# Second attention: q and k projected transposed and passed through memory into the head stacks

## The reference, cut to what matters

```python
q = input_tensor @ wq.T + bq        # k, v alike; 16 heads of 16 channels
q = q.reshape(B, S, H, D).transpose(0, 2, 1, 3)
scores = jnp.einsum('bhsd,bhtd->bhst', q, k) / jnp.sqrt(jnp.float32(D))
attn = jax.nn.softmax(scores, axis=-1)
out = jnp.einsum('bhst,bhtd->bhsd', attn, v)
out = out.transpose(0, 2, 1, 3).reshape(B, S, E)
return out @ wo.T + bo
```

## Time and profile before

| | us |
|---|---|
| time, median of 3 runs | 2039.92 (2038.96 to 2041.53) |
| profiled execution, its time | 2040.23 |
| its span | 2038.5 |
| PE busy in the span | 1894.3 (93%) |
| DVE busy | 1445.4 (71%) |
| ACT busy | 1282.9 (63%) |
| POOL busy | 648.3 (32%) |

### The profile page before, as it was taken

One profiled execution on the slowest core, in us unless ns is written; L12 is line 12 of the kernel. 1 busy time (PEld: TensorE's weight loads), 2 busy tenths in 40 slices (PEclk: granted clock), 3 DMA queues, 4 the chain that ended last, 5 costly groups with the idle time before them and its releaser, 6 DMA issues. The chain is left out here.

```text
span 2038.5 us, 33530 instructions
## 1 busy us (share of the span) xinstructions
PE 1894.3 (93%) x12080; PEld 1465.6 (72%) x12080; DVE 1445.4 (71%) x2916; ACT 1282.9 (63%) x3061; POOL 648.3 (32%) x1021
## 2 busy tenths in 40 slices
PE   1999999999999999999999789997999999999997
PEld 1888878878888888787788568885555655655653
DVE  5785885886868868858768554445777777777773
ACT  3675674665756756746657465543777677777784
POOL 0353453543543534535435413221001111111112
PEclk9999999999999999999999999996999999999999
DMA  6110211111102111111111293321001011011001
GB/s 228 42 42 22 53 42 32 42 32 43 42 22 52 42 27 47 43 32 42 32 36 41 71 335 132 109 86 52 22 1 52 1 52 52 1 52 52 1 32 42
DMA packets 75204, 111.29 MB, mean 55 GB/s; under 512 B 8224, under 2 KB 49568, under 8 KB 74528
## 3 DMA queue, kind: packets, MB, share of 16 engines
q1 hardware_dynamic: 75040, 109.14, 18.3%
HBM read 54.59 MB, written 20.97 MB: 37 GB/s over the span
## 5 line engine op out<-in xcount | busy, mean ns | idle before, releaser
L1565 DVE TENSOR_REDUCE nm<-ps 128x1 f32<-128x512 f32 x512 | 337.0, 687 | 118.5 <-PE ps L1433 114.2
L1659 ACT ACTIVATE pt<-pst 128x512 f32<-128x512 f32 x512 | 296.8, 602 | 144.5 <-PE pst L1441 143.0
L805 POOL TENSOR_SCALAR pr<-pr,rinv 128x128 f32<-128x128 f32 (+3 forms) x512 | 263.1, 533 | 373.7 <-DVE rinv L693 373.7
L573 ACT ACTIVATE pr<-sc,nmax 128x128 f32<-128x128 f32 (+3 forms) x512 | 268.1, 527 | 142.3 <-DVE nmax L682 140.9
L682 DVE TENSOR_REDUCE nmax<-sc 128x1 f32<-128x128 f32 (+3 forms) x512 | 223.0, 484 | 75.4 <-PE sc L409 75.3
L1433 PE MATMUL ps<-kb,qb 96*128 96x512 f32 x512 | 239.8, 471 | 13.5 <-DVE nm L1565 11.2
L811 POOL TENSOR_TENSOR qk<-ra,rb 128x256 f32<-128x256 f32 x256 | 183.0, 735 | 206.8 <-DVE rb L704 171.7
L1441 PE MATMUL pst<-qb,kb 128*128 128x512 f32 x512 | 208.2, 408 | 6.8 <-ACT pt L1659 3.4
L1433 PEld LDWEIGHTS ps<-kb,qb 96*128 96x128 f32 x512 | 98.7, 193 | 145.3 <-issue 84.0
L421 PE MATMUL w<-ident,pr 128*128 128x128 f32 x1280 | 170.6, 280 | 25.6 <-DVE rb L704 19.7
L383 PE MATMUL w<-wq_hi,xt_hi 128*128 128x384 f32 x512 | 183.6, 359 | 2.8 <-DVE xt_lo L676 1.5
(11 more groups left out here) (212 smaller groups left out, 4552.9 us busy)
## 6 DMA issues: line engine op xcount, KB each, us to landing
k<-k SPq DMA_DIRECT2D x256, 128.0 KB, 2.2
raw<-in_w SPq DMA_DIRECT2D x16, 640.0 KB, 5.9
raw<-in_w SPq DMA_DIRECT2D x8, 704.0 KB, 4.2
xa<-in_x SPq DMA_DIRECT2D x2, 2048.0 KB, 13.7
x<-in_x SPq DMA_DIRECT2D x8, 512.0 KB, 3.9
x_scratch<-x SPq DMA_DIRECT2D x8, 512.0 KB, 2.9
xt_hi_scratch<-xt_hi SPq DMA_DIRECT2D x1, 4096.0 KB, 14.6
xt_lo_scratch<-xt_lo SPq DMA_DIRECT2D x1, 4096.0 KB, 23.8
```

The lines of the kernel that those rows point to most:

```text
L573: act.activation(pr[:, h, SOFF[i]:SOFF[i] + (i + 1) * P], sc[:, bank, at:at + (i + 1) * P], ACT.Exp, bias=nmax[:, h, i:i + 1], accum_out=r ...
L805: pool.tensor_scalar(p, p, rinv[:, h, i:i + 1], 1.0, ALU.mult, ALU.mult).then_inc(scaled, 1)
L1565: dve.tensor_reduce(nm[:, g % 2, i, h:h + 1], ps[:, i % 2, :], AXX, ALU.max, negate=True).then_inc(max_done, 1)
L1659: act.activation(pt[:, g % 2, h, i, :], pst[:, i % 2, :], ACT.Exp).then_inc(exp_done, 1)
```

## The change

q and k are projected transposed: the weights are now the stationary operand and the tokens the moving one (`project_z`), 128 channels by 512 tokens to a piece. A piece s is q (0) or k (1) of half u of the heads; n = 2b + u counts the halves. ACT adds the bias and rounds (`round_z`), DVE makes the remainder in one instruction (`rest_z`), and SP writes each part to where it belongs in a scratch tensor `z1` in memory, six DMAs a half (`store_z`), and reads a group's stacks from there, four DMAs a group (`load_stacks`). The zero halves of `kb` are set once, on DVE and POOL ahead of the loop. v is projected as before in pieces of 256 columns (`project_v`, `take_v`). `split_z`, `turn_z`, `take_stack`, `own` and `qn` are gone. One of the two copies of the maxima goes from DVE to ACT, the selector copies too. In `experts` only q and k of the first half of batch row 0 are projected.

```diff
+def project_z(pe, c, n, s, out, xs):
+    cols = slice(s * C + n % 2 * P, s * C + n % 2 * P + P)
+    for k in range(NC):
+        pe.matmul(out, c.w1h0[:, k, cols], xs[0][:, k, :], start=(k == 0), stop=False)
+        pe.matmul(out, c.w1h0[:, k, cols], xs[1][:, k, :], start=False, stop=False)
+        mm = pe.matmul(out, c.w1l0[:, k, cols], xs[0][:, k, :], start=False, stop=(k == NC - 1))
+    mm.then_inc(c.z_done, 1)
+def round_z(act, c, n, s, src):
+    act.wait_ge(c.z_done, 2 * n + s + 1)
+    if n > 0:
+        act.wait_ge(c.z_stored, 96 * n)
+    act.activation(c.zt[:, 0, s, :], src, ACT.Identity, bias=c.bz[:, 2 * s + n % 2:2 * s + n % 2 + 1], scale=1.0).then_inc(c.zt_hi_done, 1)
+def rest_z(dve, c, n, s, src):
+    dve.wait_ge(c.zt_hi_done, 2 * n + s + 1)
+    dve.scalar_tensor_tensor(out=c.zt[:, 1, s, :], in0=src, scalar=c.bz[:, 2 * s + n % 2:2 * s + n % 2 + 1],
+                             in1=c.zt[:, 0, s, :].bitcast(F32), op0=ALU.add, op1=ALU.subtract).then_inc(c.zt_lo_done, 1)
+def store_z(sp, c, io, n):
+    for s, parts in enumerate(((0, 1, 0), (0, 0, 1))):
+        sp.wait_ge(c.zt_hi_done, 2 * n + s + 1)
+        sp.wait_ge(c.zt_lo_done, 2 * n + s + 1)
+        for r, part in enumerate(parts):
+            dst = io.z1[n % 2, s].rearrange("h (r d) t -> h r d t", d=D1)[:, r]
+            sp.dma_start(dst, c.zt[:, part, s, :].bitcast(F32)).then_inc(c.z_stored, 16)
...
-        TURNS = ((0, 0), (0, 1), (0, 3), (1, 1))
-        STACKS = ((0, 0), (0, 1), (0, 3), (1, 0), (1, 1), (1, 2))
-        PROJECTIONS = ((1, 3), (2, 0), (2, 2), (2, 3))
+        Z_PE, Z_ACT, Z_DVE = ((0, 2), (2, 0)), ((0, 3), (2, 1)), ((1, 1), (2, 2))
+        V_PE, V_DVE = ((1, 0), (1, 3), (2, 1), (2, 3)), ((1, 1), (2, 0), (2, 2), (3, 0))
+        O_PE, O_DVE = ((0, 2), (1, 1), (2, 0), (2, 3)), ((0, 3), (1, 2), (2, 1), (3, 0))
...
+                def load_stacks(q):
+                    n, g = q // 2, q % NG1
+                    sp.wait_ge(c.z_stored, 96 * n + 96)
+                    if q < NG1:
+                        sp.wait_ge(kz_pool, g + 1)
+                    else:
+                        sp.wait_ge(st_done, 16 * (q - NG1) + 16)
...
+                        sp.dma_start(qb[rows, g].bitcast(F32), zq[e]).then_inc(stack_in[g], 16)
+                        sp.dma_start(kb[rows, g].rearrange("p (a e) t -> p e a t", e=2)[:, e].bitcast(F32), zk[e]).then_inc(stack_in[g], 16)
...
+                for b in range(B):
+                    if b < B - 1:
+                        store_half(b + 1, 0)
+                        load_stacks(NG1 * (b + 1))
+                        load_stacks(NG1 * (b + 1) + 1)
+                        store_half(b + 1, 1)
+                        load_stacks(NG1 * (b + 1) + 2)
+                        if b < B - 2:
+                            load_xs(b + 2)
+                        load_stacks(NG1 * (b + 1) + 3)
+                    if b > 0:
+                        store(b - 1)
+                        load_xg(b)
...
+                            if g % 2 == 0 and (h, i) in Z_PE and not last:
+                                project_half(b + 1, g // 2, Z_PE.index((h, i)))
+                            if g == 1 and (h, i) in V_PE and not last:
+                                project_v(b + 1, V_PE.index((h, i)))
+                            if g == 3 and (h, i) in O_PE and not first:
+                                out_project(b - 1, O_PE.index((h, i)))
...
-                    for a in range(2):
-                        dve.tensor_copy(qb[2 * S3:P, g, a, :], pn[2 * D1 * a:2 * D1 * (a + 1), :]).then_inc(n_done, 1)
+                    dve.tensor_copy(qb[2 * S3:P, g, 0, :], pn[0:2 * D1, :]).then_inc(n_dve, 1)
...
+                            if g == 2 and h == 0 and i < NC and not first:
+                                split_ot(b - 1, i)
...
+                pool.memset(kb[0:2 * S3, 0, HG // 2:HG].bitcast(F32), 0.0).then_inc(kz_pool, 1)
+                for g in range(1, NG1):
+                    pool.memset(kb[0:2 * S3, g].bitcast(F32), 0.0).then_inc(kz_pool, 1)
```

More of the change, by code:

```diff
@@ L1084, in _ @@
                     ffn(e, e % 2, last=e == E1 - 1)
+                act.wait_ge(a_bias_done, 1)
+                for s in range(2):
+                    round_z(act, c, 0, s, w[:, s, :])
             @block.vector
@@ L1162, in _ @@
                     ffn(e, e % 2, last=e == E1 - 1)
[L1164 to L1169, removed]
+                for s in range(2):
+                    rest_z(dve, c, 0, s, w[:, s, :])
             @block.tensor
@@ L1384, in finish @@
                         pool.tensor_tensor(x1[:, i, :], x1[:, i, :], so[:, i % 2, :], ALU.add).then_inc(x_done, 1)
-                def row(b, first=False, last=False):
-                    for g in range(NG1):
-                        if not (last and g > 0):
-                            split_z(b + (g + 3) // NG1, (g + 3) % NG1)
-                        if g == 2 and not first:
-                            finish(b - 1)
-                for g in range(3):
-                    split_z(0, g)
                 for b in range(B):
-                    row(b, first=b == 0, last=b == B - 1)
@@ L1493, in group @@
                     back1, back2 = (not (first and g < n) for n in (1, 2))
-                    projects = g == 1 and not last
                     for h in range(HG):
@@ L1531, in group @@
+                            if h == HG - 1 and i == 1 and more1:
+                                turn_n(q + 1)
+                            if h == HG - 1 and g == 1 and not first and i >= 2:
+                                turn_on(b - 1, i - 2)
                         if back1:
                             weigh(q - 1, (g + 3) % NG1, h, b + 1 if g else b)
-                for j in range(4):
-                    turn_z(0, j, (qn_done, 2 * NT) if j < 2 else (stack_done, j - 1))
                 for n in range(HG + 1):
@@ L1641, in _ @@
                         maximum(0, 0, h, i)
+                        if h == 1:
+                            take_v(0, i)
+                        if h == 3 and i < 2:
+                            rest_z(dve, c, 1, i, w[:, i, :])
                 split_n(0, 0)
@@ L1650, in _ @@
                     take_o(q, q % NG1)
-                split_ot(B - 1)
+                for k in range(NC):
+                    split_ot(B - 1, k)
                 for i in range(NT):
@@ L1699, in group @@
                     q = NG1 * b + g
-                    more2, more3 = (not (last and g + n >= NG1) for n in (2, 3))
+                    more1 = not (last and g + 1 >= NG1)
                     back2 = not (first and g < 2)
```

304 lines of the change are left out of this document (129 added, 175 removed).

## The result

| | before | after |
|---|---|---|
| median, us | 2040.72 | 2009.99 (2008.04 to 2013.04) |
| ratio | 1 | 0.9853 [0.9841, 0.9865] |
| profiled execution, us | 2040.23 | 2010.16 |
| its span, us | 2038.5 | 2008.4 |
| DMA traffic, mean over the span | 55 GB/s | 81 GB/s |

The account below looks back on a forecast made before the run. PE looked full, but a ring of two score banks was taken to set each step's floor of 3.55 us. 2040.2 - 45.5 (seven rows) - 3.6 (last row) - 3 (start) = 1988 us, range 1966 to 2010.

Parts of the forecast that it names:

- the term of -3: Start of the attention stage: between -5 and +3 us, taken as -3, nearer to full clock.
- The round trip: Start: stacks stored to memory and loaded back, two transfers of 3 to 7 us each, for scores from about 1395.
- Wrong if PE waits for DMA in the loop: Sign against the forecast, in the attention loop: stack loads were expected hidden, about 15 us of queue against some 30.
- The clock at the start: First group at full instead of half clock, 2.5 us less, since transposes don't count as clock activity.
- the ring of two banks: Each attention step: two score banks passing between PE and the maxima set a floor of 3.55 us, not PE's work.
- Rival A: Whole loop: PE's work sets the time and every removed transpose counts, giving 1968 us, a row 67.6; chance 0.12.
- rival B: Loop: new DVE work holds up maxima, gain only 2 to 4 us a row, 2016 us; chance 0.14.
- C: Loop: stacks come late from memory; at 35 us PE waits 5 us four times a row, 2128; 0.09 with D.
- D: Loop: granted clock falls to 1.2 GHz, 14 us a group, 2044 to 2100 us; chance 0.09 together with C.
- (b): Loop: ACT loses stack copies and casts, POOL its subtractions; counted as nothing by itself.
- the 16 transposes: Each group's transposes of q and k removed: 0.56 us per bundle of four, 9.0 us of PE a batch row.
- (c): One of two casts of the maxima moves from DVE to ACT, removing a wait of 0.55 us before h=0.

Follow-up runs that it names:

- e2: Changed kernel with project_z of batch row 0's first half moved into the last expert's down projection and its stores ahead of the last gate stores: 2008.54 us.
- e4: Changed kernel with the edits of e1 and e2 together: 1993.0 us, ratio 0.9765.
- e3: Changed kernel with k's three of the six first-half z stores issued from ACT's queue instead of SP's: 2009.09 us, ratio 0.9845.
- e7: Changed kernel with scratch rows reordered so the 128 rows of a z store lie at one pitch, not in 8 blocks: 2000.45 us.
- e8: Changed kernel with the edits of e1, e2 and e7, and each gate store cut in two of 64 rows: 1982.55 us, ratio 0.9715.
- e9: As e8, but with project_z of batch row 0 left behind the last down projection: 1981.26 us, ratio 0.9715.
- e1: Changed kernel with load_xs(1) issued on SP's queue ahead of row 0's second-half stores and the stacks of groups 2 and 3: 1997.17 us.
- e10: Kernel before, with ACT copying only 8 of 512 columns of each q and k stack from the fifth group on: 2030.96 us, ratio 0.9952.
- e6: Kernel before, with only one of four transposes in each q and k bundle made from the third group on: 2025.76 us, ratio 0.9929.
- e5: Changed kernel with both casts of the maxima on DVE again, none on ACT: 2019.73 us, ratio 0.9899.

## Why the prediction was right and where it was wrong

**The step that failed is the start, the term of -3, measured +20.4.** Some 1.2 us of it were there before the stage (its first projection starts at 1378.05 before and at 1379.24 after). That is within what single executions differ by: e2 and e4 are the same kernel up to there, and their first store comes at 1378.59 and 1381.01. The rest has two parts.

- *The round trip.* "I let the stage end where it does", scores "from about 1395". First score at 1406.38: 11.4 us later than forecast, 7.1 later than before. I counted the transfers as two, one behind the other, at 3 to 7 us each, taken from loads and an output store. The second is that: 5.9 us from the first load's issue to the first score. But the first is six stores of 256 KB, and from the first of them to the first load it is 16.4 us (1384.12 to 1400.53). Their rate, 147 GB/s behind gate stores at 30 to 48, also set the stage's end. e2 and e3 ruled out the place of the projection and the issuing queue, e7, e8 and e9 showed the shape of the stores. In e9, with the first load at 1389.17 instead of 1400.53, the first score comes at 1394.84, about what I had forecast for the change, and both transfers take 5.7 us. So 3 to 7 us hold for stores of that shape, and not for those of the change.
- *The input of row 1.* I weighed SP's queue in the middle of the loop, where 30 us of slack stood against 15, and found it hidden; so it is. At the start the same order has no slack: 13.96 us, shown by e1 (-15.1 at the marker); the sum had no term for it. This fault could have been seen without a chip: `load_xs(1)` stands behind `load_stacks(3)` (e1's diff), and PE's program wants it in the first h = 0. "Wrong if PE waits for DMA in the loop" came true there, in the loop's first group, and only there.

The sum goes by three stretches of PE: the first score is 7.1 us later than before (the 1.2 are in it); from there to the first transposed score it is 21.2 us against 20.6, +0.6; from there to the marker 34.1 against 21.4, +12.7, which is the 14.0 of the wait less 1.3 for the rest of the first group. 7.1 + 0.6 + 12.7 = 20.4. In e9, where neither fault is left, the time from the first transposed score (1415.70) to the marker is 19.85 us against 21.40 before; 2.5 less had been predicted, 1.55 came. The first transposed score itself, forecast at 1417.5 to 1421.5, came at 1427.55, for the lateness of the first score. POOL's work was priced too high and set nothing: the clearing of `kb`, forecast at 10 us from a memset of 2.89 us, took 6.2, and the same memset of `vs` takes 1.80 us in after; the maxima waited for the first score.

**The clock at the start went as argued, and was worth little.** Before, PE is granted 0.56 while busy for 7.16 of 7.20 us. "Largely with transposes" says too much: they are 15 of the 26 matmuls in it and 3.41 us of the busy time. After, PE gets 1.00 in 1415 to 1420 with projections and scores, busy for 4.85 of 5.00 us (the window stands above, at e7). That is the direction of what the prediction cites from the Trainium skill on transposes; but no run changes only the transposes of the start, so it is not shown that they are the cause. And 0.62 follows at once, in 1421.1 to 1432.3, where PE is busy for 6.74 of 11.20 us and waits for the rest, so the full clock was had for a part of the start only. In e9, where neither fault is left, the first group gave 1.55 of the 2.5 us put on the full clock; the start as a whole came to -5.7 there.

**The loop, term by term.** Forecast for a middle row 70.05, measured 69.79; from the marker to the end -45.5 - 3.6 = -49.1 forecast, -50.5 measured. These are -47.3 up to the last row, -4.4 in it (59.65 against 64.10), and +1.2 behind it, where no term stood: from the last weigh to the end of the span it is 20.02 us before (the first of the two fences below) and 21.25 after, with a granted clock of 0.88 before and 0.74 after; the last output projection's matmuls start 0.12 us apart before and mostly 0.21 after.

```profile
2018.48:2038.50 20.02, 9.14 (x72) 5.73 (x72) 4.35 (x10) 1.66 (x3) 5.68 (x8) 0.88 0.08 27
```

```profile
1987.15:2008.40 21.25, 11.48 (x72) 7.93 (x72) 4.45 (x10) 1.75 (x3) 5.68 (x8) 0.74 0.23 74
```

Step by step, in a middle row:

| step | forecast | measured |
|---|---|---|
| g=0, h=0 to 3 | 4.9, 3.95, 4.75, 4.0 | 4.81, 3.85, 4.83, 3.71 |
| g=1 | 4.4, 5.0, 4.5, 4.4 | 4.19, 4.92, 4.59, 4.38 |
| g=2 | 4.9, 3.95, 4.75, 4.0 | 4.99, 3.86, 4.82, 3.72 |
| g=3 | 4.05, 4.2, 4.6, 3.7 | 4.12, 4.23, 4.83, 3.95 |

The floor of 3.55 us by the ring of two banks, with the holes filled by the work put into them, held in all 16 steps within 0.3 us. Rival A, PE's issue work alone, asked for 67.6; rival B for 73 and more; C for waits for the stacks, of which the list of waits behind the marker has none, D for a lower clock than the 1.00 of the middle rows. Two prices that had no row in before came out as follows in 1668.03 to 1737.82 (count, busy us, mean ns, idle before):

```profile
L877 DVE SCALAR_TENSOR_TENSOR zt<-w1a,bz,zt 128x512 fp32r<-128x512 f32 x4 | 3.0, 747 | 0.3 <-ACT zt L872 0.2
...
L872 ACT ACTIVATE zt<-w1a,bz 128x512 fp32r<-128x512 f32 x4 | 2.7, 681 | 0.0
```

747 ns where I took 690, and 681 where I took 600; both beside PE's work, and neither moved the sum.

**Right in the sum, wrong in a cause.** Of (b), ACT's work, the prediction says "so this counts nothing by itself". e10 says that ACT's copies are worth 9 us over the kernel: three of a row's four h=0 steps get shorter by 0.34 to 0.38 us (5.28 to 4.94 for one), which is 1.1 a row and 7.5 in seven rows. And what I gave to the 16 transposes, 0.56 a bundle, is partly theirs: e6's middle row, without three quarters of the transposes, is only 1.9 us shorter (74.71), where 9.0 us were counted for all of them. A ladder for that step: 5.28 before; 4.94 without the copies, 4.97 without three quarters of the transposes; 4.55 without both; and by an estimate 3.6 if the casts' stall (0.56) and the last quarter of the transposes (a quarter of 3 x 0.56, 0.4) go too, beside the 3.7 that I had put for a bare h=0 and the 3.81 that the last row's h=0 of g=0 takes in after. So the end of the ladder was right since it was counted from the floor up; the steps on the way there, from 5.28 down, were not, and that they didn't spoil the sum is luck. (c), the second cast, holds, at 0.3 us a group (e5) and not 0.55.

What stays open: how much of the loop's gain is the new places of the projections, and why the clock is lower behind the last weigh.

## What to carry to other kernels

Predict a software-pipelined loop from its floor, then the first turn as a case of its own: walk through every queue in program order and ask for each issue what it stands behind and who wants it first. The detour through memory was hidden in this loop and exposed in full at its start; its price there was the rate of the stores, and that depended on the shape of the access. Look at the DMA share and the GB/s of the stretch: here shares of 0.46 and of 0.10 to 0.14 stood beside stores with 8 and with 2 blocks outermost, and with the same bytes in another shape the share rose to 0.76 and 0.82.

## What the runs showed of the hardware

- Six stores of 256 KB with 8 blocks outermost took 10.39 us (behind the gate stores) and 6.35 us of issue, at 140 to 147 GB/s; the same bytes with 128 rows at one pitch took 3.29 us (e9, with the gate stores cut too) and 3.10 us (e7), at 286 to 298 GB/s.
- The z stores took 1.1 (after, second half) to 2.8 us (e3) each of their queue's time, the loads of the stacks behind them 0.43; a second issuing queue (e3) left the first load at 1399.99, against 1400.53.
- Transposes on PE and copies on ACT of the same data, in the same step, gave gains that add (14 us and 9 us alone, 25 together).
